# All places of the work in a transformer block's rounds set anew (steady rounds, opening, last batch)

## The chip, the cores and the metric

One NeuronCore of a Trainium2 chip (trn2). The metric is the device time of one execution in microseconds (us); several executions are timed and the median is given. Beside them stands one profiled execution, from which all rows below are taken.

## What is computed

The input x has 16 batches of 512 rows of 128 channels. A feed-forward layer, an attention layer and the same feed-forward layer follow each other, each on the normalised rows and each added to its input:

```
x = x + 0.5 * ffn(layernorm(x))
x = x + attn(layernorm(x))
x = x + 0.5 * ffn(layernorm(x))

ffn(x)  = x @ quantize_int4(kernel) + bias + (x @ a) @ b
attn(x) : 16 heads of 64; keys and values from a latent of 32 channels,
          causal mask, softmax over the 512 keys, projection back to 128
```

The feed-forward weights are folded into one 128x128 matrix before the first batch. The query and key products of a head are folded into a 128x32 matrix, so that a score is a product with the latent, and split into a high and a low part in fp32r.

## The kernel before, in words

The five engines run programs of their own, each a loop over rounds t = -2 to 16. A round has 44 places, u = 0 to 43. In a steady round every engine works on four batches at once:

- **the scores of batch t**: at each place TensorE makes one score block (`score(u)`, lines L912 and L916) into one of two PSUM banks, and ScalarE takes its exponential (L748), `e0` to `e43`. Score u waits until exponential u - 2 has freed its bank. TensorE then weighs the latents with the exponentials (`weigh_latents`, L952, 16 steps g, j), and sums rows for the denominators (L925, `weigh_ones`); GpSimd adds the exponentials of a group of heads ahead of that (`add_probs`, L625).
- **the row maxima of batch t + 1**: 38 units v (`max_unit`, L988 on TensorE into a ring of three banks, L1244 on VectorE, 0.6 us each); two of them, half of the heads each, end in a transpose (L973, L1234) and a DMA of 32x128 values into the query stack (`place_max`, L451). The scores of a half wait for that DMA.
- **the front of batch t + 2**: nine units of the first feed-forward layer, norms, keys and queries (`front_unit`, L1018 to L1035), each into the one bank `aux`. Units 4 to 7 make the queries of four groups of heads. Of each, ScalarE copies the high part (`front_copy`, L782) and VectorE takes the low part (`q_low`, L1351). When the second group is done (place `LOW_AT[3]`), the queue of SyncE issues 12 DMAs that stack these queries (`stack_queries(0)`, L419), and then, in its own order, `place_max(0)` for the next round's first score.
- **the tail of batch t - 1**: denominators inverted and spread (L1272, L1279), the scaling on GpSimd (L632), four projections (`project_out`, L1079) into `aux`, the sum with the first layer's output on VectorE (L1325, place `TAIL_SUM_AT`), its statistics (L1218 and L1224, place `TAIL_STATS_AT`), a transpose and a product (`tail_unit`, L1092 and L1095), and the output (L1332).

`aux` is used in turn by the front units, the projections and the tail units. Each user waits for the one before it to be read out. The first projection (place `PROJECT_AT[0]`) waits for front unit 4's low part (place `LOW_AT[2]`), and front unit 5 waits for the tail's sum.

Each piece has its place from tables of numbers at the head of the file; every engine runs through u = 0 to 43 and issues what has that place, in a fixed order within a place. A place of 44 or more lies in the next round. Nothing reorders this at run time: an instruction that waits holds all behind it on its engine. The tables have three sets: for steady rounds, for the opening (rounds -2 and -1, names with OPENING and FIRST), and for the last batch (names with LAST).

In the opening, round -1 makes the maxima units of batch 0 (33 of 38) beside the front of batch 1; after each unit a filler matmul runs (`keep_awake`, L1042). GpSimd takes the low parts there. ScalarE writes mask rows into the second query stack in four copies (`mask_queries`, L717, places `MASK_AT`), and the first score of batch 0 waits for all of them. The last batch has no other batch beside it: in round 16 only its last weighings, its denominators and its tail are left (`closing` on VectorE). Every `weigh_ones` that is placed in round 16 first waits for the last exponential and runs four filler matmuls (`stay_busy_by_columns`, L1063).

Of the kernel before, what the change touches and what calls it, by code (L numbers as in the profile page):

```python
# [112 lines left out]
def nth(par):  # L113

    return DMA // 2, DMA - DMA // 2 * par


def scores_by(s):
# [7 lines left out]
    8, 8, 8, 10, 11, 11, 13, 14, 15, 15, 17, 18, 19, 20, 21, 23, 23, 24, 28, 28, 29, 31, 32, 33, 34, 35, 36, 37, 37,  # L126
    38, 39, 39, 40, 42, 44, 45, 45, 50]
FIRST_MAX_AT = [
    4, 4, 4, 4, 6, 11, 11, 12, 12, 12, 12, 16, 16, 18, 18, 19, 19, 19, 23, 23, 25, 25, 28, 32, 34, 34, 36, 36, 39,
    40, 40, 41, 42, 44, 45, 46, 46, 50]  # L130
FRONT_AT = [1, 4, 12, 16, 19, 30, 33, 37, 41]
PROJECT_AT = [21, 22, 25, 27]
TAIL_AT = [35, 43]
WEIGH_AT = [[9, 9, 9, 13], [17, 21, 21, 21], [32, 34, 34, 34], [47, 50, 50, 50]]
ONES_AT = [21, 34, 50, 50]
# [5 lines left out]
FRONT_ACT_AT = [3, 7, 13, 17, 20, 31, 34, 38, 42]  # L141
NORM_AT = [9, 9, 9, 9]
TAIL_ACT_AT = 36
READ_AT = [16, 30, 37, 50]

SUM_AT = 4
STATS_AT = 6
LOW_AT = [14, 17, 21, 31, 34, 39]
TAIL_SUM_AT = 27
TAIL_STATS_AT = 28  # L150
OUT_AT = 43
NEXT_STATS_AT = 21
INVERT_AT = 6
SPREAD_AT = [8, 9, 14, 18]

SCALE_AT = [14, 15, 22, 22]
ADD_AT = [[7, 9, 19], [27, 30, 30], [41, 41, 44], [45, 46, 48]]
FIRST_RSTD_AT = 28
RSTD_AT = 4
TAIL_RSTD_AT = 34  # L160
BIAS_AT = 1
TAIL_BIAS_AT = 30


OPENING_FRONT_AT = [0, 2, 6, 13, 18, 19, 27, 36, 41]
OPENING_FRONT_ACT_AT = [0, 9, 22, 30, 32, 35, 37, 40, 41]
OPENING_NORM_AT = [8, 12, 13, 14]
OPENING_SUM_AT = 1
OPENING_STATS_AT = 3
OPENING_LOW_AT = [25, 26, 27, 30, 37, 38]  # L170
OPENING_NEXT_STATS_AT = 24
OPENING_FIRST_RSTD_AT = 40
OPENING_RSTD_AT = 7
OPENING_BIAS_AT = 4

LAST_ADD_AT = [[10, 22, 22], [22, 24, 25], [28, 29, 34], [40, 40, 42]]
# [33 lines left out]
def macaron_block(nc, x, wq, wkv_down, wk_up, wv_up, wout, ffn_w, ffn_bias, ffn_a, ffn_b, out):  # L210
    ctx = ExitStack()
    with ctx:
# [301 lines left out]
        def _(pool):  # L514
# [59 lines left out]
            def one_round(t, par):  # L574
# [76 lines left out]

                for u in range(SCORES):
# [22 lines left out]
                    if is_first(t) and u == 0:  # L675
                        pool.wait_ge(bias_loaded, DMA)
                        nc.gpsimd.tensor_scalar(half_bias[:], half_bias[:], 0.5, None, ALU.mult).then_inc(const_made, 1)
                        pool.wait_ge(const_made, 7)
                    if prep and u == bias_at:
                        wait_batch(pool, f_full, t, 2, F_UNITS, 1)  # L680
                        nc.gpsimd.tensor_tensor(x_in[:, par], x_in[:, par], half_bias[:, None, :].broadcast_to([P, TT, D]),
                                                ALU.add).then_inc(xb_made, 1)
# [4 lines left out]
                    if end and u == TAIL_BIAS_AT:  # L687
                        first = 0
                        if not attend:
                            first = TT - 1  # L690
                            pool.wait_ge(x2_closed, first)
                            wait_batch(pool, out_stored, t, -1, DMA, 0)
                            nc.gpsimd.tensor_tensor(x2b[:, 0:first], x2[:, 0:first],
                                                    half_bias[:, None, :].broadcast_to([P, first, D]), ALU.add).then_inc(x2b_begun, 1)
                            pool.wait_ge(x2b_begun, 1)
                        wait_batch(pool, t_free, t, -1, T_UNITS, 1)
                        wait_batch(pool, out_stored, t, -1, DMA, 0)
                        nc.gpsimd.tensor_tensor(x2b[:, first:], x2[:, first:], half_bias[:, None, :].broadcast_to([P, TT - first, D]),
                                                ALU.add).then_inc(x2b_made, 1)
# [4 lines left out]
        def _(act):  # L704
# [27 lines left out]
            def one_round(t, par):  # L732
# [67 lines left out]

                for u in range(SCORES):
                    if t == -1 and u in MASK_AT:
                        mask_queries(1, MASK_AT.index(u))
                    if end and u == TAIL_ACT_AT:
                        wait_batch(act, t_full, t, -1, T_UNITS, 2)
                        nc.scalar.activation(x2_t[:], aux[:], ACT.Copy).then_inc(t_free, 1)
# [334 lines left out]
        def _(dve):  # L1141
# [67 lines left out]
            def one_round(t, par):  # L1209
# [101 lines left out]
                for u in range(SCORES):  # L1311
                    if prep and u == sum_at:
                        wait_batch(dve, f_full, t, 2, F_UNITS, 2)
                        wait_batch(dve, xb_made, t, 2, 1, 1)
                        wait_batch(dve, x1_saved[par], t, 0, *nth(par))
                        wait_batch(dve, f_rstd_made, t, 2, 2, 1)
                        for i in range(TT):
                            last = nc.vector.scalar_tensor_tensor(x1[:, par, i, :], aux[:, i * P:(i + 1) * P],
                                                                  f_rstd[:, 0, i:i + 1], x_in[:, par, i, :],
                                                                  ALU.mult, ALU.add)  # L1320
                        last.then_inc(f_free, 1)
# [91 lines left out]
```

## Time and profile before

| | |
|---|---|
| three timed runs, us | 785.49, 784.26, 780.52; median 784.26 |
| the profiled execution, us | 784.9 |
| its span from first to last instruction, us | 783.2 |
| mean granted TensorE clock | 0.984 of 2.4 GHz |
| TensorE matmul busy | 764.2 us, 98% |
| VectorE / ScalarE / GpSimd busy | 80% / 65% / 83% |

The span can be read as an opening up to about 62 us (the first score), 14 rounds with all or nearly all four stages, and a last part without a next batch from about 730 us. Steady rounds take some 45 us each. Matmuls are pipelined and their ends are modelled, so busy matmul time also holds short waits between them.

### The profile page before, as it was taken

How to read it: one execution, taken by the hardware profiler on the slowest of the kernel's cores; microseconds unless marked ns; L12 is line 12 of the kernel's file. 1: busy time of each engine (PE TensorE's matmuls, PEld its weight loads, DVE VectorE, ACT ScalarE, POOL GpSimd, SP SyncE). 2: the span in 40 equal slices, each digit the busy share in tenths (PEclk: the TensorE clock that was granted, in tenths of full speed). 3: DMA queues.
4: the chain of work that ended last, by engine and by line, in shares of the span. 5: the costliest groups of instructions: out<-in, count | busy, mean ns of one | idle time of the engine just before them, and what ended most of it. 6: DMA issues, size and time to landing. Idle time of an engine off the chain costs nothing.

```text
span 783.2 us, 20715 instructions
## 1 busy us (share of the span) xinstructions
PE 764.2 (98%) x7632; PEld 591.6 (76%) x7632; DVE 623.7 (80%) x1983; ACT 507.5 (65%) x995; POOL 650.0 (83%) x449
## 2 busy tenths in 40 slices
PE   8799999999999999999999999999999999999997
PEld 6687777777787778778787877878787777867665
DVE  4678788788878888898878879887887889776635
ACT  6277676667667676767657666676766676655670
POOL 5626788898899989888998989889898988888892
PEclk7789999999999999999999999999999999999999
DMA  5647270734636172553627154372616445360101
GB/s 117 159 98 173 58 181 25 163 86 106 148 80 147 47 159 73 123 130 82 164 48 162 50 134 120 84 169 61 148 47 150 101 110 130 75 150 3 30 1 42
DMA packets 81141, 80.99 MB, mean 103 GB/s; under 512 B 16064, under 2 KB 68560, under 8 KB 81040
## 3 DMA queue, kind: packets, MB, share of 16 engines
q1 hardware_dynamic: 80480, 78.47, 43.0%
q10 hardware_dynamic: 560, 1.20, 0.6%
q8 instruction: 61, 1.00, 0.5%
q14 instruction: 40, 0.33, 0.1%
HBM read 9.90 MB, written 8.39 MB: 23 GB/s over the span
## 4 chain that ended last, share of the span: by engine, by line
PE 79%; SPq 7%; DVE 6%; DMA 2%; ACT 2%; issue 2%; POOL 1%; DVEq 0%; POOLq 0%; ACTq 0%
PE bank L952 16%; PE bank L988 14%; PE bank L916 12%; PE bank L925 7%; PE bank L912 7%; PE bank L1079 7%; SPq L419 7%; DMA q_stack<-max_t 2%; PE bank L1021 2%; PE bank L1018 2%; PE bank L1030 2%; PE bank L1032 2%; PE bank L1031 2%; PE bank L1095 1%; PE bank L1042 1%
## 5 line engine op out<-in xcount | busy, mean ns | idle before, releaser
L1244 DVE TENSOR_REDUCE strip_max<-bank 128x8 f32<-128x512 f32 (+1 forms) x384 | 254.1, 683 | 51.6 <-PE bank L988 50.7
L748 ACT ACTIVATE later_probs<-bank 128x512 f32<-128x512 f32 x384 | 216.3, 601 | 65.5 <-PE bank L916 41.0
L748 ACT ACTIVATE first_probs<-bank 128x384 f32<-128x384 f32 (+1 forms) x320 | 157.5, 513 | 137.0 <-PE bank L916 69.5
L625 POOL TENSOR_TENSOR totals<-totals,later_probs 128x1024 f32<-128x1024 f32 x124 | 227.6, 1835 | 12.5 <-ACT later_probs L748 0.4
L625 POOL TENSOR_TENSOR totals<-first_probs,later_probs 128x1536 f32<-128x1536 f32 x62 | 215.6, 3478 | 26.1 <-ACT later_probs L748 26.1
L988 PE MATMUL bank<-keys,q_stack 118*128 118x512 f32 (+7 forms) x1024 | 215.1, 303 | 1.8 <-DVE maxima L1244 1.7
L916 PE MATMUL bank<-q_stack,keys 119*128 119x384 f32 (+1 forms) x448 | 185.2, 422 | 2.4 <-ACT later_probs L748 1.3
L988 PEld LDWEIGHTS bank<-keys,q_stack 118*128 118x128 f32 x1024 | 177.1, 191 | 12.6 <-DVE maxima L1244 2.2
L1244 DVE TENSOR_REDUCE maxima<-bank 128x1 f32<-128x512 f32 (+1 forms) x192 | 128.1, 681 | 2.1 <-PE bank L988 1.9
L912 PE MATMUL bank<-q_stack,keys 119*128 119x256 f32 x512 | 114.0, 304 | 2.8 <-DMA q_stack<-max_t 2.6
L916 PEld LDWEIGHTS bank<-q_stack,keys 119*128 119x128 f32 x448 | 82.7, 188 | 44.9 <-ACT first_probs L748 16.2
L912 PEld LDWEIGHTS bank<-q_stack,keys 119*128 119x128 f32 x512 | 82.4, 189 | 33.3 <-ACT later_probs L748 17.2
L952 PE MATMUL bank<-later_probs,lat 128*32 128x384 f32 (+2 forms) x1536 | 99.9, 383 | 0.0
L632 POOL TENSOR_TENSOR y_norm<-y_sb,y_norm 128x512 f32<-128x512 f32 x60 | 76.7, 1291 | 15.6 <-DVE y_norm L1279 15.6
L952 PEld LDWEIGHTS bank<-later_probs,lat 128*32 128x32 f32 x1536 | 43.1, 109 | 53.5 <-issue 35.1
L1079 PE MATMUL bank<-w_out,y_norm 128*128 128x128 f32 x512 | 69.1, 278 | 1.3 <-POOL y_norm L614 1.3
L1079 PEld LDWEIGHTS bank<-w_out,y_norm 128*128 128x128 f32 x512 | 63.1, 191 | 5.7 <-issue 3.8
L952 PE MATMUL bank<-first_probs,lat 128*32 128x512 f32 x512 | 66.7, 593 | 0.3 <-ACT y_sb L754 0.2
L1279 DVE STREAM_SHUFFLE y_norm<-den_inv 128x128 f32<-128x128 f32 x240 | 54.2, 308 | 0.5
L925 PE MATMUL bank<-totals,row_ones 128*32 128x128 f32 x1512 | 50.4, 273 | 0.0
L754 ACT ACTIVATE y_sb<-bank 128x512 f32<-128x512 f32 x64 | 38.4, 601 | 16.9 <-PE bank L952 16.9
L1351 DVE TENSOR_TENSOR q_low<-bank,q_high 128x512 fp32r<-128x512 f32 x60 | 41.0, 684 | 9.1 <-ACT q_high L782 9.1
(157 smaller groups left out, 917.0 us busy)
## 6 DMA issues: line engine op xcount, KB each, us to landing
q_stack<-q_high SPq DMA_DIRECT2D x252, 128.0 KB, 2.4
q_stack<-q_low SPq DMA_DIRECT2D x128, 128.0 KB, 2.4
x_in<-in_L_attn_x_bld_dram SPq DMA_DIRECT2D x16, 256.0 KB, 3.3
out_dram<-x SPq DMA_DIRECT2D x16, 256.0 KB, 3.5
x_back<-out_dram SPq DMA_DIRECT2D x16, 256.0 KB, 3.0
out_dram<-x2b SPq DMA_DIRECT2D x15, 256.0 KB, 2.3
keys<-keys_staged SPq DMA_DIRECT2D x16, 192.0 KB, 2.9
keys<-keys_staged SPq DMA_DIRECT2D x32, 96.0 KB, 2.6
```

The lines of the kernel that those rows point to most:

```text
L419: eng.dma_start(dst.bitcast(F32), src[e * LD:(e + 1) * LD, half].rearrange("c w o q -> c (w o q)").bitcast(F32)).then_inc(q_stacked[half][ ...
L625: nc.gpsimd.tensor_tensor(total, first_probs[g % 2][:, :, P:] if j == 1 else total, probs_of(g, j)[:], ALU.add).then_inc(added, 1)
L632: nc.gpsimd.tensor_tensor(y_norm[:, g, :], y_sb[:, g, :], y_norm[:, g, :], ALU.mult).then_inc(y_normed, 1)
L748: nc.scalar.activation(out, score_bank(t, u)[:, 0:heads * cols].rearrange("p (e q) -> p e q", e=heads), ACT.Exp).then_inc(exp_done, 1)
L912: last = nc.tensor.matmul(out, strips(par, KM, OWN[w]), q_stack[par][:, pair:pair + HG, w, of, :], start=True, stop=True)
L916: last = nc.tensor.matmul(bank[:, 0:heads * (n - P)], strips(par, KM, LATER[j]), q_stack[par][:, pair + e:pair + e + heads, 2 * (j + 1):SU ...
L925: last = nc.tensor.matmul(den_bank[e * LD:(e + 1) * LD, 0:P], row_ones[:, row:row + LD], of[:, e, :], start=start, stop=stop)
L952: last = nc.tensor.matmul(y_bank[e * LD:(e + 1) * LD, j * P:L], lat[(par + off) % 2][:, j, :], probs_of(g, j)[:, e, 0:L - P * j], start=(j ...
L988: last = nc.tensor.matmul(bank[:, col:col + n], queries, strips((par + off) % 2, KC, SEEN[w]), start=True, stop=True)
L1079: last = nc.tensor.matmul(out_tile(t, i), y_norm[:, g, i * P:(i + 1) * P], w_out[:, g, :], start=(g == 0), stop=(g == G - 1))
L1244: nc.vector.tensor_reduce(out, bank[:].rearrange("q (b k) -> q b k", k=strip), AX.X, ALU.max).then_inc(a_free, 1)
L1279: last = nc.vector.stream_shuffle(y_norm[:, g, i * P:(i + 1) * P], den_inv[:], [g * TT + i] * LD)
```

## The change

The tables of places get new numbers, for steady rounds, opening and last batch. Beside them some code is put into functions of its own (`add_front`, `add_tail`, `make_out`, `take_low`, `front_stats`, `tail_stats` on VectorE, `halve_bias`, `add_bias`, `tail_bias` on GpSimd, `tail_copy` on ScalarE), which are called from the same points with the same waits, so that the line numbers of the kernel after are some 12 to 25 higher. The lines of the tables of which the prediction speaks:

```diff
-FRONT_AT = [1, 4, 12, 16, 19, 30, 33, 37, 41]
-PROJECT_AT = [21, 22, 25, 27]
+FRONT_AT = [2, 4, 11, 15, 19, 29, 32, 37, 41]
+PROJECT_AT = [23, 25, 26, 27]
...
-LAST_WEIGH_AT = [[10, 13, 13, 14], [21, 21, 25, 31], [33, 40, 40, 40], [42, 50, 51, 52]]
-LAST_ONES_AT = [33, 40, 49, 54]
+LAST_WEIGH_AT = [[8, 14, 14, 14], [20, 24, 24, 24], [30, 37, 37, 37], [55, 61, 62, 66]]
+LAST_ONES_AT = [37, 45, 65, 92]
...
-MASK_AT = [23, 31, 36, 37]
+MASK_AT = [16, 21, 30, 34]
...
-LOW_AT = [14, 17, 21, 31, 34, 39]
-TAIL_SUM_AT = 27
-TAIL_STATS_AT = 28
+LOW_AT = [14, 16, 21, 30, 34, 39]
+TAIL_SUM_AT = 28
+TAIL_STATS_AT = 32
...
-NEXT_STATS_AT = 21
+NEXT_STATS_AT = 20
...
-OPENING_FRONT_AT = [0, 2, 6, 13, 18, 19, 27, 36, 41]
+OPENING_FRONT_AT = [2, 5, 9, 20, 24, 25, 27, 29, 39]
...
-LAST_ADD_AT = [[10, 22, 22], [22, 24, 25], [28, 29, 34], [40, 40, 42]]
+LAST_ADD_AT = [[16, 21, 31], [31, 32, 32], [35, 35, 40], [43, 60, 61]]
```

The moved code keeps its form, as here on VectorE:

```diff
                 for u in range(SCORES):
                     if prep and u == sum_at:
-                        wait_batch(dve, f_full, t, 2, F_UNITS, 2)
...
-                        last.then_inc(f_free, 1)
+                        add_front()
```

**First place: VectorE in a steady round, between the tail's sum and the low part of the second query group.** `x<-bank,x_back` is the sum, BN_STATS and BN_AGGR of `t_stats` are its statistics, TENSOR_REDUCE are maxima units, `q_low` is the low part on which SyncE's queue waits. Before:

```order
L1325 TENSOR_TENSOR x<-bank,x_back 128x512
L1244 TENSOR_REDUCE maxima<-bank 128x1
L1244 TENSOR_REDUCE strip_max<-bank 128x8
L1218 BN_STATS t_stats<-x 128x6 x4
L1224 BN_AGGR t_mv<-t_stats 128x2 x4
L1244 TENSOR_REDUCE strip_max<-bank 128x4
L1351 TENSOR_TENSOR q_low<-bank,q_high 128x8x64
```

And after, the same stretch (the sum is L1343 there, the low part L1374):

```order
L1343 TENSOR_TENSOR x<-bank,x_back 128x512
L1260 TENSOR_REDUCE strip_max<-bank 128x8
L1260 TENSOR_REDUCE strip_max<-bank 128x4
L1374 TENSOR_TENSOR q_low<-bank,q_high 128x8x64
L1260 TENSOR_REDUCE strip_max<-bank 128x8
L1250 TENSOR_SCALAR max_t<-bank 32x128
L1260 TENSOR_REDUCE maxima<-bank 128x1
L1234 BN_STATS t_stats<-x 128x6 x4
L1240 BN_AGGR t_mv<-t_stats 128x2 x4
```

One maxima unit now stands ahead of the sum, and the eight instructions of the statistics stand behind the low part.

**Second place: VectorE in a steady round, ahead of the first projection.** `f_stats<-x_in` are the input statistics of batch t + 3, the `q_low` here is that of the first query group, for which the first projection waits. Before:

```order
L1279 STREAM_SHUFFLE y_norm<-den_inv 128x128 x4
L1244 TENSOR_REDUCE strip_max<-bank 128x8
L1244 TENSOR_REDUCE maxima<-bank 128x1
L1351 TENSOR_TENSOR q_low<-bank,q_high 128x8x64
L1244 TENSOR_REDUCE strip_max<-bank 128x8
L1218 BN_STATS f_stats<-x_in 128x6 x4
L1224 BN_AGGR f_mv<-f_stats 128x2 x4
```

And after:

```order
L1260 TENSOR_REDUCE strip_max<-bank 128x8
L1295 STREAM_SHUFFLE y_norm<-den_inv 128x128 x4
L1260 TENSOR_REDUCE maxima<-bank 128x1
L1234 BN_STATS f_stats<-x_in 128x6 x4
L1240 BN_AGGR f_mv<-f_stats 128x2 x4
L1374 TENSOR_TENSOR q_low<-bank,q_high 128x8x64
L1260 TENSOR_REDUCE strip_max<-bank 128x8
```

The statistics stand ahead of the low part instead of behind it. On TensorE the first projection moves back too, behind two more scores and two maxima units.

**Third place: TensorE in round -1, around the transposes of the normalised rows** (`bank<-identity,xn`, front unit 2 of batch 1). `keys,q_stack` are maxima units of batch 0, `bank<-identity` is a filler matmul. Before:

```order
L988 MATMUL bank<-keys,q_stack 128x512
L1042 MATMUL bank<-identity 128x128
L1018 MATMUL bank<-identity,xn 128x128 x4
L988 MATMUL bank<-keys,q_stack 128x448
L988 MATMUL bank<-keys,q_stack 128x64
L1042 MATMUL bank<-identity 128x128
L988 MATMUL bank<-keys,q_stack 128x384
L988 MATMUL bank<-keys,q_stack 128x128
```

And after:

```order
L1004 MATMUL bank<-keys,q_stack 128x512
L1058 MATMUL bank<-identity 128x128
L1004 MATMUL bank<-keys,q_stack 128x448
L1004 MATMUL bank<-keys,q_stack 128x64
L1058 MATMUL bank<-identity 128x128
L1004 MATMUL bank<-keys,q_stack 128x384
L1004 MATMUL bank<-keys,q_stack 128x128
L1058 MATMUL bank<-identity 128x128
L1034 MATMUL bank<-identity,xn 128x128 x4
```

Two maxima units stand ahead of the transposes instead of behind them.

In the last batch, the row sums of group 1 and the first weighing of group 3 stand in round 15 before, and in round 16 after; so two `weigh_ones` lie in round 16 instead of one, each with its four filler matmuls.

## Rows read from the trace of the kernel before

**Rows 1.** The page's part 1: busy us, share of the span, instructions of an engine.

```profile
PE 764.2 (98%) x7632; PEld 591.6 (76%) x7632; DVE 623.7 (80%) x1983; ACT 507.5 (65%) x995; POOL 650.0 (83%) x449
```

**Rows 2.** The chain of waits, whole span: start us, us, what; one same step per round.

```profile
107.88 1.42 PE bank L925 x48
...
423.62 1.31 PE bank L925 x48
...
468.44 1.50 PE bank L925 x48
...
513.93 1.31 PE bank L925 x48
...
693.26 1.31 PE bank L925 x48
```

**Rows 3.** The chain of waits from 355 to 373 us, the end of a steady round.

```profile
355.60 0.91 PE bank L1079 x8
...
356.53 0.69 DVE x L1325
...
358.42 0.79 DVE t_stats L1218 x4
...
359.34 0.38 DVE t_mv L1224 x4
...
360.21 0.69 DVE q_low L1351
...
363.53 1.59 SPq L419
...
369.68 2.29 DMA q_stack<-max_t
...
372.02 0.50 PE bank L912 x2
```

**Rows 4.** Who waited for whom on TensorE, whole span: us in total, times, longest.

```profile
PE bank L912 <- DMA q_stack<-max_t: 2.6, 7, 0.8
```

**Rows 5.** Instructions in order of time, 348.5 to 352.5 us: start, us, engine.

```profile
349.58 0.68 DVE L1351 TENSOR_TENSOR q_low<-bank,q_high 128x512 fp32r<-128x512 f32 x1
...
350.68 1.16 PE L1079 MATMUL bank<-w_out,y_norm 128*128 128x128 f32 x8
350.78 0.86 DVE L1218 BATCH_NORM_STATS2 f_stats<-x_in 128x6 f32<-128x128 f32 x4
...
351.78 0.62 DVE L1224 BATCH_NORM_AGGREGATE f_mv<-f_stats 128x2 f32<-128x6 f32 x4
```

**Rows 6.** Instructions in order of time, opening, 36 to 62 us.

```profile
39.33 1.54 PE L1018 MATMUL bank<-identity,xn 128*128 128x128 f32 x4 [0.91 <-ACT xn L761]
...
41.34 0.69 DVE L1244 TENSOR_REDUCE strip_max<-bank 128x8 f32<-128x512 f32 x1 [1.91 <-PE bank L988]
...
48.01 1.91 ACT L717 ACTIVATE q_stack<-first_probs 22x2048 fp32r<-22x2048 f32 x1
...
49.94 0.60 ACT L782 ACTIVATE q_high<-bank 128x512 fp32r<-128x512 f32 x1
...
54.56 1.15 SPq L419 DMA_DIRECT2D q_stack<-q_high  x2
...
61.67 0.48 PE L912 MATMUL bank<-q_stack,keys 119*128 119x256 f32 x2
```

**Rows 7.** Busy us of each engine in two stretches of the opening, then PEclk.

```profile
35.00:40.00 5.00, 2.37 (x13) 1.59 (x11) 4.25 (x14) 1.31 (x4) 1.69 (x4) 0.86 0.94 211
40.00:45.00 5.00, 5.00 (x21) 4.66 (x21) 2.77 (x4) 3.33 (x4) 1.27 (x1) 0.50 0.82 203
```

**Rows 8.** Instructions in order of time, last batch, 761 to 769 us.

```profile
763.39 0.60 ACT L748 ACTIVATE later_probs<-bank 128x512 f32<-128x512 f32 x1 [0.54 <-PE bank L912]
...
764.18 1.07 PE L1063 MATMUL bank<-w_out,identity 128*32 128x512 f32 x8
...
768.35 0.96 DVE L1272 RECIPROCAL den_inv<-bank 128x128 f32<-128x128 f32 x1 [2.94 <-PE bank L925]
```

More of the change, by code:

```diff
@@ L687, in one_round @@
                     if end and u == TAIL_BIAS_AT:
[L688 to L699, printed above, removed]
+                        tail_bias()
             rounds(pool, one_round)
@@ L799, in front_copy, with tail_copy @@
                                              ACT.Copy).then_inc(f_free, 1)
+                def tail_copy():
+                    wait_batch(act, t_full, t, -1, T_UNITS, 2)
+                    nc.scalar.activation(x2_t[:], aux[:], ACT.Copy).then_inc(t_free, 1)
                 for u in range(SCORES):
@@ new lines, in add_front @@
+                def add_front():
+                    wait_batch(dve, f_full, t, 2, F_UNITS, 2)
+                    wait_batch(dve, xb_made, t, 2, 1, 1)
+                    wait_batch(dve, x1_saved[par], t, 0, *nth(par))
+                    wait_batch(dve, f_rstd_made, t, 2, 2, 1)
+                    for i in range(TT):
+                        last = nc.vector.scalar_tensor_tensor(x1[:, par, i, :], aux[:, i * P:(i + 1) * P],
+                                                              f_rstd[:, 0, i:i + 1], x_in[:, par, i, :],
+                                                              ALU.mult, ALU.add)
+                    last.then_inc(f_free, 1)
@@ new lines, in add_tail, with make_out @@
+                def add_tail():
+                    wait_batch(dve, t_full, t, -1, T_UNITS, 1)
+                    wait_batch(dve, x1_loaded, t, -1, DMA, DMA)
+                    nc.vector.tensor_tensor(x2[:].rearrange("p i d -> p (i d)"), aux[:],
+                                            x1_back[:].rearrange("p i d -> p (i d)"), ALU.add).then_inc(t_free, 1)
+                def make_out():
+                    wait_batch(dve, t_full, t, -1, T_UNITS, 3)
+                    wait_batch(dve, x2b_made, t, -1, 1, 1)
+                    wait_batch(dve, t_rstd_made, t, -1, 1, 1)
+                    for i in range(TT):
+                        last = nc.vector.scalar_tensor_tensor(x2b[:, i, :], aux[:, i * P:(i + 1) * P],
+                                                              t_rstd[:, i:i + 1], x2b[:, i, :], ALU.mult, ALU.add)
+                        if not attend and i == TT // 2 - 1:
+                            last.then_inc(half_out, 1)
+                    last.then_inc(t_free, 1)
@@ L1340, in one_round @@
                                                 ALU.subtract).then_inc(f_free, 1)
-                    if prep and not low_by_pool(t) and u == low_at[1]:
+                    elif n == 1:
                         wait_batch(dve, kh_made, t, 2, 1, 1)
```

148 lines of the change are left out of this document (77 added, 71 removed).

## The prediction, made before the result was known

> **What bounds the kernel now.** I read the page's engine totals first. TensorE's matmuls are busy 98% of the span [rows 1], the next engines 83% and 80%. A reader should see two things: no other engine is the bound over the whole, and only some 19 us without a matmul are left (783.2 less 764.2). Then the chain of waits over the whole span. It goes along TensorE nearly everywhere, and one step of it, the row sums of group 0, comes back once per round [rows 2]. From the first to the last of these rows it is 693.26 - 107.88 = 585.38 us for 13 rounds, 45.03 us each. The rounds aren't alike: 468.44 - 423.62 = 44.82, and the next one 513.93 - 468.44 = 45.49. So there is a round in which hardly anything is waited for, and 13 such rounds would take 582.7, 2.7 us less than now.
>
> What the others wait for stands in the chain at the end of a round [rows 3]. It leaves TensorE at the last projection (ends 356.51), goes over VectorE's sum, the statistics of that sum and the low part of the second query group (ends 360.90), then over 12 DMA issues in SyncE's queue to 369.68, where the maxima's DMA is issued. That takes 2.29, and the first score of the next round starts at 372.02. The list of waits gives this one 2.6 us in 7 rounds on TensorE [rows 4]. It is TensorE's longest entry, and small: order can win little in steady rounds, unless it shortens what TensorE does itself.
>
> The page on traces speaks on this. By the Trainium skill (Perfetto Trace Analysis, Identifying the Most-Contended Engine) matmul occupancy says little of the headroom, and weight loads are the better measure. Here those are 76% against 98% [rows 1]. By the one number 19 us are left to win in all, by the other far more; I let the waits decide, not either share.
>
> **The change, steady rounds.** The set of matmuls of a round stays as it is, so TensorE's own work doesn't change, and only waits can.
>
> - *The low part of query group 2 comes earlier.* Before, sum (starts 356.53), two maxima units, statistics, one unit, low part. The statistics take 358.42 to 359.72, 1.30 us [rows 3]; they now stand behind. A maxima unit moves ahead of the sum, where VectorE waits for the projection anyhow: another 0.60 (357.82 to 358.42 is one unit, from the same rows). The last projection comes one unit later on TensorE (0.24). That makes 1.30 + 0.60 - 0.24 = 1.66 at most; the high copy by ScalarE will then be what comes last, so I take 1.3, between 1.0 and 1.66. SyncE's 12 issues (8.8 us, one of them 1.59 instead of 0.59) and the DMA follow 1.3 us earlier. The longest excess of a round is 45.49 - 44.82 = 0.67, so the first score no longer waits: -2.7.
> - *The first front unit stands one score later* (`FRONT_AT[0]`). It needs `aux`, which the output of the round before reads until shortly after the new round's first score. A round that starts without the wait above meets this one. No row prices it; I bound it by 0 and by one score, 0.2 us a round, and take 0.1 times 13: -1.3.
> - *The input statistics stand ahead of the low part for which the first projection waits.* That low part ends at 350.26 and the projection starts at 350.68 [rows 5], so 0.42 us of cover. The statistics run 350.78 to 352.40, with a wait inside; without it they are as the others, 1.30. Low part: 350.26 + 1.30 + 0.1 = 351.7, to 351.9 with the wait. The projection stands behind two more scores and two more units (some 0.4 + 0.24 + 0.2 + 0.24 = 1.1 us): 351.8. So between 0 and 0.15 us a round, I take 0.05, times 13: +0.6.
> - The tail's statistics, now later, are needed by the output only, at the round's end; GpSimd's root for it has 8 us. The bias add on GpSimd comes behind one more addition (2.4 us), and the front sum behind one more weighing (0.65): the norms after it wait 0.8 us longer at most, and ScalarE has exponentials to do there. The new groups of weighings on TensorE have as many changes between small and large matmuls as the old. Nothing for these, 0 to 0.1 us a round.
>
> Steady rounds: -2.7 - 1.3 + 0.6 = **-3.4** (bounds -5.3 to -0.7).
>
> **The opening.** From 37 to 62 us VectorE's maxima units, 0.6 us each, are the longest chain, and it has gaps. The longest is 1.91 us [rows 6]: TensorE waits for the norms (0.91) with the transposes, and the next maxima unit stands behind them. Two units now stand ahead: two of 0.6 fit in the gap, -1.2. Between the transposes and the next front unit one unit less stands, which brings ScalarE's copies forward. There a mask copy of 1.91 runs until 49.92 and the query copy behind it starts at 49.94 [rows 6], though its matmuls had ended some 0.5 us before; that mask copy moves behind the next front units: -0.5. The rest is what the following front units, each waiting for ScalarE to free `aux`, gain by being earlier; I add 0.8 (0 to 1.5). Then the first score would start 2.5 earlier, at 59.2 instead of 61.67. There a new limit stands: of the four mask copies three now lie between and behind the query copies, and the last ends about 59.2 by the same durations. Hence **-2.5** (0 to -4). The queue of SyncE, which starts its 12 issues at 54.56 when the third low part is there, goes the same 1.6 us or more earlier, so that batch 1's keys are not late.
>
> The clock in this stretch: 2.37 of 5 us busy, then 0.50 granted, that is 1.2 GHz [rows 7]. By the Trainium skill (TensorE: Matmul & The Clock Gate, Part 1) it is idleness that halves the clock, and the trace agrees. The stretch before it doesn't change, so I leave this as it is.
>
> **The last batch.** Work is moved from round 15 into 16: row sums of group 1 and the first weighing of group 3. ScalarE's last exponentials come earlier, since GpSimd's additions and the weighings no longer hold them: I reckon some 3 us before the 763.39 of now [rows 8]. But TensorE has then 0.65 + 1.9 of moved work and four more filler matmuls (1.07 us, rows 8) left behind the last exponential. 3.0 against 3.6 less some overlap: **0** (-2 to +1.5). From the last denominators (VectorE at 768.35) on, nothing changes.
>
> **Sum.** The profiled execution took 784.9 (span 783.2 and 1.7 around it): 784.9 - 3.4 - 2.5 + 0 = 779.0. It lies 0.6 above the median of the runs, 784.26, so against that median I say 778.4.
>
> **The rivals.**
>
> *The first projection waits (slower).* VectorE gets to the low part of the first query group later than I say: besides the statistics its high copy stands behind one more exponential. The trace is for it in that my margin is 0.1 us; against it, that VectorE has idle time in every round (80% busy). It costs from the first 0.1 us on, in each of 13 rounds, and makes the kernel slower than before from 5.9 / 13 = 0.45 us. With all of the 1.30 uncovered less the present 0.42 cover and more of the same, 1.0 a round: 778.4 + 13 = 791.4.
>
> *The wait goes and the rounds stay as long.* ScalarE works without a gap at a round's end, and TensorE is held there by exponentials; an earlier first score is then given back a few us later. For it: a round without the wait at its start was not the shortest. Against: 44.82 was reached several times. Steady rounds then give 0.5, the opening its 2.5: 784.9 - 3.0 - 0.6 = 781.3.
>
> *TensorE's clock stays up in the opening.* Two more units at 38.5 to 40 us. If they kept the clock at 2.4 GHz, the 5 us of full work at half clock [rows 7] would take about 2.5, of which VectorE lets 2.2 through: 776.2. Against it: the fall comes behind a stretch that doesn't change.
>
> *The rounds get shorter than the shortest now.* The order also takes away waits too short to be listed, in scores that wait for exponentials. 0.3 a round times 13: 778.4 - 3.9 = 774.5. For it: a matmul's modelled end hides such waits in the 98%.
>
> **How the numbers follow.** Forecast (776 to 781) 0.44; projection waits 0.09; rounds stay 0.20; clock 0.12; shorter rounds 0.15. Likeliest time 778.4. For 8 in 10 the range runs from the shorter rounds with something of the opening, 773, to beyond the case in which rounds stay as they are, 784; most of the first rival is left out. A measurement of this kernel can tell about 1% from no change, 7.8 us, so faster means under 776.4 and slower over 792.1. Faster: the last two rivals and the edge of the forecast, 0.27 + 0.06 = 0.33. Slower: most of the first rival, 0.07. Within 1%: 0.60.
>
> **What would show it right or wrong.** In the profile after: the wait of the first score for the maxima's DMA is gone from TensorE's list; the recurring step of the chain comes every 44.7 to 44.8 us; SyncE's queue is no longer in the chain of steady rounds; the first projection shows at most 0.1 us behind VectorE's low part. The first score starts at 59 to 60 us, right behind the last mask copy. In the last batch the last exponential starts about 3 us earlier against the start of its round, and the last denominators don't. Wrong would be: rounds over 45.0 with a new entry for the projection, or a first score at 61 or later.

## The result, and the profile after

| | before | after |
|---|---|---|
| median of 13 timed runs, us | 782.67 (780.52 to 787.65) | 777.19 (775.72 to 782.57) |
| ratio after to before | | 0.9937, 95% interval 0.9913 to 0.996 |
| span of the profiled execution, us | 783.2 | 774.5 |
| its mean granted TensorE clock | 0.984 | 0.995 |

The time fell by 5 to 5.5 us, 0.6% (0.4 to 0.9%): inside the band of 1% that the prediction called no change, 1.2 us from the predicted 778.4. A second measurement of the changed kernel (seven executions, beside 21 of the kernel before) gave 777.77 against 783.5, ratio 0.9933 (0.9909 to 0.9957). The profiled executions differ by more, 8.7 us, and a part of that is luck of the clock (below). So where the clock matters, before is compared with the profile of the second measurement (span 777.6): up to 38 us its clock ran as that of before.

The page's part 1 of the kernel after, as [rows 1]:

```profile
PE 758.5 (98%) x7638; PEld 586.5 (76%) x7638; DVE 624.6 (81%) x1983; ACT 508.3 (66%) x995; POOL 649.6 (84%) x449
```

Six matmul records more (eight for the fillers of the second `weigh_ones` in round 16, two of `keep_awake` less), and still 98%: the shares say nothing on what was gained. The chain's shares by engine, from the page's part 4, first of before and then of after, do:

```profile
PE 79%; SPq 7%; DVE 6%; DMA 2%; ACT 2%; issue 2%; POOL 1%; DVEq 0%; POOLq 0%; ACTq 0%
```

```profile
PE 93%; DVE 3%; ACT 2%; POOL 1%; issue 1%; DVEq 0%; POOLq 0%; ACTq 0%
```

SyncE's queue and the DMA have left the chain: the end of a round no longer runs over the stacking of queries. The recurring step, in the chain of waits of after (start us, us, what; [rows 2] before):

```profile
102.09 1.31 PE bank L941 x48
147.03 1.31 PE bank L941 x48
191.89 1.31 PE bank L941 x48
...
684.85 1.31 PE bank L941 x48
726.24 1.31 PE bank L941 x48
```

Thirteen rounds take 684.85 - 102.09 = 582.76, 44.83 each (before 45.03), and nearly every one 44.86 (191.89 - 147.03, for one; the step before round 14 is 43.93, since maxima and front run out there). Before, the shortest full rounds took 44.82 and the longer ones up to 45.81; now nearly all are like the shortest, but none of the full rounds is shorter than 44.84. Experiment 3 shows why not. TensorE's longest waits after, total, times, longest:

```profile
PE bank L1095 <- POOL y_norm L614: 1.3, 2, 0.7
PE bank L846 <- POOL neg_half L517: 1.2, 1, 1.2
```

The entry of [rows 4], the first score waiting for the maxima's DMA, isn't there. The end of the steady round, in order of time on VectorE, ScalarE and SyncE's queue ([rows 3] in chain form before):

```profile
349.75 0.69 DVE L1343 TENSOR_TENSOR x<-bank,x_back 128x512 f32<-128x512 f32 x1 [0.20 <-PE bank L1095]
350.35 1.28 DVE L1260 TENSOR_REDUCE strip_max<-bank 128x8 f32<-128x512 f32 x2
351.56 0.60 ACT L794 ACTIVATE q_high<-bank 128x512 fp32r<-128x512 f32 x1
352.19 0.69 DVE L1374 TENSOR_TENSOR q_low<-bank,q_high 128x512 fp32r<-128x512 f32 x1 [0.55 <-ACT q_high L794]
...
353.05 1.15 SPq L419 DMA_DIRECT2D q_stack<-q_high  x2
...
361.78 0.53 SPq L451 DMA_DIRECT2D q_stack<-max_t  x1
```

From the sum to the low part it is now 2.44 us (352.19 - 349.75) against 3.68 before (360.21 - 356.53), 1.24 less. VectorE idles 0.55 ahead of the low part for ScalarE's high copy, so that copy is what comes last now.

**Where the time came from.** The recurring step cuts both spans into the same pieces (before, and the second profile of after). Opening to the first score: 61.67 and 58.31, -3.4. From there to the first such step: 46.21 and 47.06, +0.9. Thirteen rounds: 585.38 and 582.63 (105.37 to 688.00), -2.8. Round 14: 42.02 and 41.40, -0.6. The rest: 47.92 and 48.2, +0.3. Together -5.6, the difference of the spans. Of the -3.4, about 0.9 is clock and not order: between the normalisation of batch 1 and the first score TensorE ran 6.8 us at half clock before and 3.4 in the second profile of after, and in the old opening 6.8 instead of 3.4 made 0.94 (22.98 and 22.04, experiment 4).

### The profile page after: what moved, and what is told of

Same layout as the page of the kernel before. It is cut to its first block, busy times and chain, and to the rows that moved or that the text cites. A ratio compares the mean times of both kernels' runs of the same rounds, so it can differ in the third digit from the quotient of the medians.

```text
span 774.5 us, 20727 instructions
## 1 busy us (share of the span) xinstructions
PE 758.5 (98%) x7638; PEld 586.5 (76%) x7638; DVE 624.6 (81%) x1983; ACT 508.3 (66%) x995; POOL 649.6 (84%) x449
## 4 chain that ended last, share of the span: by engine, by line
PE 93%; DVE 3%; ACT 2%; POOL 1%; issue 1%; DVEq 0%; POOLq 0%; ACTq 0%
PE bank L968 19%; PE bank L1004 18%; PE bank L932 15%; PE bank L928 9%; PE bank L941 8%; PE bank L1095 7%; PE bank L1046 3%; PE bank L1048 2%; PE bank L1047 2%; PE bank L1034 2%; PE bank L1037 2%; PE bank L1111 2%; PE bank L1108 1%; ACT later_probs L760 1%; PE bank L1051 1%
## 5 line engine op out<-in xcount | busy, mean ns | idle before, releaser
L1260 DVE TENSOR_REDUCE strip_max<-bank 128x8 f32<-128x512 f32 (+1 forms) x384 | 249.9, 682 | 17.3 <-PE bank L1004 16.3
L760 ACT ACTIVATE first_probs<-bank 128x384 f32<-128x384 f32 (+1 forms) x320 | 150.8, 511 | 105.1 <-PE bank L932 70.5
L1004 PE MATMUL bank<-keys,q_stack 118*128 118x512 f32 (+7 forms) x1024 | 212.6, 305 | 1.9 <-DVE maxima L1260 1.0
L932 PE MATMUL bank<-q_stack,keys 119*128 119x384 f32 (+1 forms) x448 | 177.3, 419 | 1.3 <-ACT first_probs L760 0.8
L1004 PEld LDWEIGHTS bank<-keys,q_stack 118*128 118x128 f32 x1024 | 168.7, 190 | 10.8 <-DVE maxima L1260 1.7
L928 PE MATMUL bank<-q_stack,keys 119*128 119x256 f32 x512 | 111.8, 301 | 0.3 <-ACT later_probs L760 0.2
L968 PE MATMUL bank<-later_probs,lat 128*32 128x384 f32 (+2 forms) x1536 | 104.8, 383 | 0.0
L1095 PE MATMUL bank<-w_out,y_norm 128*128 128x128 f32 x512 | 68.4, 277 | 1.7 <-POOL y_norm L614 1.3
L1095 PEld LDWEIGHTS bank<-w_out,y_norm 128*128 128x128 f32 x512 | 64.3, 191 | 4.9 <-issue 2.2
L1374 DVE TENSOR_TENSOR q_low<-bank,q_high 128x512 fp32r<-128x512 f32 x60 | 40.8, 679 | 7.6 <-ACT q_high L794 7.5
```

Source lines behind the costliest of these rows:

```text
L760: nc.scalar.activation(out, score_bank(t, u)[:, 0:heads * cols].rearrange("p (e q) -> p e q", e=heads), ACT.Exp).then_inc(exp_done, 1)
L928: last = nc.tensor.matmul(out, strips(par, KM, OWN[w]), q_stack[par][:, pair:pair + HG, w, of, :], start=True, stop=True)
L932: last = nc.tensor.matmul(bank[:, 0:heads * (n - P)], strips(par, KM, LATER[j]), q_stack[par][:, pair + e:pair + e + heads, 2 * (j + 1):SU ...
L968: last = nc.tensor.matmul(y_bank[e * LD:(e + 1) * LD, j * P:L], lat[(par + off) % 2][:, j, :], probs_of(g, j)[:, e, 0:L - P * j], start=(j ...
L1004: last = nc.tensor.matmul(bank[:, col:col + n], queries, strips((par + off) % 2, KC, SEEN[w]), start=True, stop=True)
L1095: last = nc.tensor.matmul(out_tile(t, i), y_norm[:, g, i * P:(i + 1) * P], w_out[:, g, :], start=(g == 0), stop=(g == G - 1))
```

## The experiments

Each variant is compared with executions of the kernel before (or of the changed kernel, 777.77) on the same chip; "13 rounds" is the length between the first and the 14th recurring step of its profile.

**1. The steady tables alone, and the opening tables alone.** The kernel before with the new MAX, FRONT, PROJECT, LOW, TAIL, ADD and other steady tables, but the old ones for opening and last batch:

```diff
-FRONT_AT = [1, 4, 12, 16, 19, 30, 33, 37, 41]
+FRONT_AT = [2, 4, 11, 15, 19, 29, 32, 37, 41]
...
-TAIL_STATS_AT = 28
+TAIL_STATS_AT = 32
```

> The kernel before with the new steady tables alone; opening and last batch keep their old places. If the steady part of the gain is the first score's wait for the maxima's DMA, that wait is gone from TensorE's list, each round takes about 44.85 us as in the kernel after, the 13 rounds from group 0's row sums to the last of them take about 583.3 instead of 585.4 us, and the time falls by 2.0 to 2.8 us. Rival, that the whole gain is made in the opening: rounds as in the kernel after, but nothing of it at the end, within 0.5 us of before. Rival, that the tables only work together: slower than before by 1 us or more.

Measured: 781.99 against 782.33, ratio 0.9995 (0.997 to 1.002), so between 2.3 us less and 1.6 more: the 2.0 to 2.8 us expected aren't to be seen in the time, though its rounds are as expected. The second kernel takes only the opening's tables and `MASK_AT`:

```diff
-MASK_AT = [23, 31, 36, 37]
+MASK_AT = [16, 21, 30, 34]
...
-OPENING_FRONT_AT = [0, 2, 6, 13, 18, 19, 27, 36, 41]
+OPENING_FRONT_AT = [2, 5, 9, 20, 24, 25, 27, 29, 39]
```

> The kernel before with the new opening tables alone. If the opening's order is worth 2.5 us by itself, the first score starts 2.5 us earlier than in a run of before with the same clock in its first 50 us, and the time falls by 2 to 3 us; the 13 steady rounds take 585 to 586 us as before. Rival, that the first score at 55.4 us after against 61.7 before was the clock of the two profiled executions and nothing else: time within 0.5 us of before over the rounds, and the first score anywhere from 55 to 62 us. Rival, that the order is worth the whole 6.6 us: time 6 us less.

Measured: 779.14 against 782.33, ratio 0.9966 (0.9939 to 0.9994). So the opening is worth something by itself, between 0.5 and 4.8 us. Its 13 rounds take 584.46, 0.9 less than before, and TensorE still lists the first score's wait:

```profile
PE bank L912 <- DMA q_stack<-max_t: 1.7, 4, 0.9
```

The steady tables give their gain in the rounds (688.35 - 105.71 = 582.64 in the first kernel), and lose part of it ahead of them (first score at 58.75 to the first such step 46.96, before 46.21) and in the last batch. From the first score of the last batch to VectorE's last denominators, the rows of the steady-only kernel, of after, and of before are these:

```profile
723.65 0.48 PE L912 MATMUL bank<-q_stack,keys 119*128 119x256 f32 x2
...
764.06 0.96 DVE L1272 RECIPROCAL den_inv<-bank 128x128 f32<-128x128 f32 x1 [2.94 <-PE bank L925]
```

```profile
720.15 0.48 PE L928 MATMUL bank<-q_stack,keys 119*128 119x256 f32 x2
...
759.62 0.96 DVE L1288 RECIPROCAL den_inv<-bank 128x128 f32<-128x128 f32 x1 [3.45 <-PE bank L941]
```

```profile
729.09 0.48 PE L912 MATMUL bank<-q_stack,keys 119*128 119x256 f32 x2
```

That is 40.41, 39.47 and, with [rows 8], 39.26. New steady tables with the old last batch cost 1.15; the new last tables bring 0.94 of it back. Their worth is a repair. The new last weighings and row sums in the kernel before, with nothing else moved, gave no time: that kernel deadlocks, with engines left waiting for the denominators. So the last batch has no measurement of its own.

**2. One number alone: the tail's statistics.**

```diff
-TAIL_STATS_AT = 28
+TAIL_STATS_AT = 32
```

> The kernel before with one number changed, TAIL_STATS_AT 28 to 32: the tail's statistics stand behind the low part of the second query group. If the chain sum, statistics, low part, 12 issues, DMA, first score is what made rounds uneven, this alone takes the wait away: no wait of TensorE for the maxima's DMA, every round 44.8 to 44.9 us, the 13 rounds 582.8 to 583.5 us, time 2.0 to 2.8 us less. Rival, that ScalarE's end of the round holds TensorE anyway: the wait moves, the 13 rounds stay at 585 us.

Measured: 793.21 against 782.33, ratio 1.0128 (1.0078 to 1.0178). Slower by 10 to 11 us, which no theory had. Its lists of waits lead to the cause: TensorE's longest entry, then GpSimd's, then the same pair in the kernel before:

```profile
PE bank L925 <- POOL totals L625: 9.2, 13, 1.0
```

```profile
POOL t_var L582 <- DVE t_mv L1224: 46.6, 16, 4.4
```

```profile
POOL t_var L582 <- DVE t_mv L1224: 5.0, 13, 1.3
```

GpSimd takes the root of these statistics at place `TAIL_RSTD_AT` (34), ahead of additions that TensorE's row sums need. Nothing overtakes a waiting instruction, so GpSimd stood up to 4.4 us before the root in each round, and the additions behind it came late, as its rows in order of time show:

```profile
367.00 0.23 POOL L582 TENSOR_SCALAR t_var<-t_mv 128x4 f32<-128x4 f32 x1 [2.91 <-DVE t_mv L1224]
367.31 1.04 POOL L584 TENSOR_TENSOR t_rstd<-t_var,neg_half 128x4 f32<-128x4 f32 x1
...
368.32 3.49 POOL L625 TENSOR_TENSOR totals<-first_probs,later_probs 128x1536 f32<-128x1536 f32 x1
```

The change moves that root to 42, behind the additions that have place 41. So the two numbers belong together, and a run took both.

```diff
-TAIL_STATS_AT = 28
+TAIL_STATS_AT = 32
...
-TAIL_RSTD_AT = 34
+TAIL_RSTD_AT = 42
```

> The kernel before with TAIL_STATS_AT 28 to 32 and, this time, TAIL_RSTD_AT 34 to 42 with it, so that GpSimd's root no longer holds the additions. Theory A (the loss of 11.7 us in the run with the statistics alone came from the root held in front of the additions): the loss is gone, the low part of the second query group stands some 0.6 us earlier than before (as the variant of the changed kernel with the statistics set back showed with the other sign), the wait of the first score is mostly gone, rounds of 44.6 to 44.9, 13 of them 582 to 583.5, so 2 to 3 us less than before, about 780.5. Theory B (the later statistics themselves make the rounds long): rounds stay near 45.7, 793.

Measured: 779.87 against 782.02, ratio 0.9973 (0.9954 to 0.9993); 13 rounds in 582.41 (106.25 to 688.66), 2.97 less than before. The recurring step in its chain:

```profile
106.25 1.42 PE bank L925 x48
...
688.66 1.31 PE bank L925 x48
```

Theory A holds: two numbers give as much in the 13 rounds as all steady tables together. The other way round, in the changed kernel:

```diff
-TAIL_STATS_AT = 32
+TAIL_STATS_AT = 29
```

> The changed kernel with TAIL_STATS_AT set back from 32 to 29, so that the tail's statistics (1.3 us) stand ahead of the low part of the second query group again; GpSimd's root stays late (42). Theory of the prediction (the statistics ahead of the low part make SyncE's queue and with it the maxima's DMA late): the low part is 1.0 to 1.3 us later, the wait of the first score is back in part of the rounds (0.2 to 0.7 us each), 2 to 3 us more than the changed kernel. Rival (the root's place on GpSimd made the wait, since it held the additions): the time stays.

Measured: 777.8 beside 777.77 of the changed kernel; 13 rounds in 583.06, 0.30 more. The expected 2 to 3 us didn't come back, and by the time alone this is what the rival said. The rows say more. The low part starts 3.68 behind the sum before, 3.15 in the kernel with the pair, 3.11 here and 2.44 in the changed kernel. So the statistics alone move it by 0.53 or 0.67, and not by their own 1.3. The first score's weight load (engine PEld) waits for the maxima's DMA accordingly, in the kernel before, with the pair, and here:

```profile
PEld bank L912 <- DMA q_stack<-max_t: 3.9, 7, 1.0
```

```profile
PEld bank L912 <- DMA q_stack<-max_t: 0.7, 4, 0.2
```

```profile
PEld bank L928 <- DMA q_stack<-max_t: 0.5, 2, 0.3
```

In the changed kernel the entry is missing. Less than half of the lead already takes most of the wait away; the rest buys little. The root at 42 with the statistics still at 28 wasn't run, so a share of the root in the 2.97 isn't excluded. Against a large one speaks that TensorE's weight loads waited only 0.4 us for GpSimd's additions before, and 0.4 with the pair.

**3. The two moves that the prediction priced at 0.1 and 0.05 a round.** In the changed kernel, each for itself:

```diff
-NEXT_STATS_AT = 20
+NEXT_STATS_AT = 21
```

> The changed kernel with one number set back: NEXT_STATS_AT 20 to 21, so that the input statistics stand behind the low part of the first query group again. Theory A (this move makes the first projection wait in every round, about 0.2 us, since the shortest round grew from 44.65 to 44.85): rounds of 44.65, 13 x 0.2 = 2.6 us less than the changed kernel, about 774.5 us. Theory B (the 0.2 a round is something else, such as one weighing more that changes tile size): rounds stay at 44.85, same time within 0.5 us.

Measured: **774.16** (773.29 to 775.93) beside 777.77 (776.61 to 779.78); ratio to before 0.9884 (0.9856 to 0.9912). Theory A holds: 13 rounds in 579.93 (103.23 to 683.16), 2.83 less than after (expected 2.6). The medians differ by 3.6, but all six executions of this kernel had a mean clock of 0.993 or more and only four of the seven beside it did; against those four (median 777.1) it is 3.0. Nearly every round now takes 44.63, which is shorter than the shortest full round before (44.82). So in the changed kernel this move had eaten what the first front unit (below) gave, and that is why none of its rounds fell under 44.84.

Round 0, though, grew: from the first score to the first recurring step it is 47.63, in after 47.05.

The chain around the first projection (L1095 x8), in after and then in this kernel:

```profile
342.87 0.66 PE bank L941 x24
...
344.43 0.23 PE bank L1004 x2
344.66 1.13 PE bank L1095 x8
```

```profile
342.90 0.66 PE bank L941 x24
...
344.45 0.23 PE bank L1004 x2
344.69 0.92 PE bank L1095 x8
```

The step takes 1.13 instead of 0.92. No wait is listed for it: at 0.2 us a round it hides as a longer step, and in the timeline as a weight load that comes 0.17 late:

```profile
343.90 0.66 DVE L1374 TENSOR_TENSOR q_low<-bank,q_high 128x512 fp32r<-128x512 f32 x1
...
344.63 0.97 PEld L1095 LDWEIGHTS bank<-w_out,y_norm 128*128 128x128 f32 x8 [0.17 <-issue]
```

The low part ends at 344.56 and the load starts at 344.63; with the number set back the load starts at 344.44. "issue" names no releaser; the time beside the low part's end, and the run with the low part moved, do.

```diff
-FRONT_AT = [2, 4, 11, 15, 19, 29, 32, 37, 41]
+FRONT_AT = [1, 4, 11, 15, 19, 29, 32, 37, 41]
```

> The changed kernel with FRONT_AT[0] set back from 2 to 1: the first front unit stands behind the round's first score again and may wait for aux, which the output reads. The prediction gave this move 0.1 us a round (between 0 and 0.2), so it expects rounds of 44.95 and 1.3 us more than the changed kernel. Rival: the output is read out by then, and the move is worth nothing: 44.85 and the same time.

Measured: 778.53 beside 777.77; 13 rounds in 687.23 - 102.55 = 584.68, 1.92 more, 0.15 a round. The rival (worth nothing) is out by the rounds; the medians alone wouldn't tell it. The chain shows the wait at the front unit's transposes (L1034) as a step of 0.07 and a longer step, here and then in after:

```profile
322.21 0.07 issue
322.28 0.63 PE bank L1034 x4
```

```profile
321.34 0.51 PE bank L1034 x4
```

A last run tried to keep the 0.22 a round without the loss that place 21 brought in round 0:

```diff
-                next_stats_at = OPENING_NEXT_STATS_AT if t < 0 else NEXT_STATS_AT
+                next_stats_at = OPENING_NEXT_STATS_AT if t < 0 else 20 if t == 0 else NEXT_STATS_AT
```

> The changed kernel with NEXT_STATS_AT 21 (the version that won 0.22 us a round), but 20 in round 0, where the place 21 made the round 0.58 us longer (40.62 against 40.04). Expected: 13 rounds of 580.8 as there, round 0 back at 40.04, so 3.3 us less than the changed kernel, 773.6 us. Rival: round 0 gives it back in round 1, and it is 774.2 as there.

Measured: 775.19 (773.49 to 778.6) against 782.02, ratio 0.9917 (0.989 to 0.9944). 13 rounds take 579.67 (105.69 to 685.36), and from the first score (58.53) to the first recurring step it is 47.16, so round 0 came back and round 1 (44.74) didn't take it. But the timed runs don't set it apart from the simpler version.

**4. Inside the opening.** First, the two maxima units ahead of the transposes, and nothing else (`FIRST_MAX_AT`, two numbers):

```diff
-    4, 4, 4, 4, 6, 11, 11, 12, 12, 12, 12, 16, 16, 18, 18, 19, 19, 19, 23, 23, 25, 25, 28, 32, 34, 34, 36, 36, 39,
+    4, 4, 4, 4, 6, 6, 6, 12, 12, 12, 12, 16, 16, 18, 18, 19, 19, 19, 23, 23, 25, 25, 28, 32, 34, 34, 36, 36, 39,
```

> The kernel before with two maxima units of the opening (units 5 and 6 of batch 0) moved ahead of the transposes on TensorE, nothing else. The prediction gave this 1.2 us: the gap of 1.91 us on VectorE shrinks to 0.7, and the first score comes 1.2 earlier. Rival (ScalarE's copies and the front units that wait for them are the chain, and the maxima only fill): the gap shrinks to about 1, but the first score comes 0 to 0.5 us earlier.

Measured: 782.04 against 782.02, ratio 0.9984 (0.9958 to 1.001): not to be told from nothing by time. Then the opening tables with the mask copies left at their old places:

```diff
 MASK_AT = [23, 31, 36, 37]
...
-OPENING_FRONT_AT = [0, 2, 6, 13, 18, 19, 27, 36, 41]
+OPENING_FRONT_AT = [2, 5, 9, 20, 24, 25, 27, 29, 39]
```

> The kernel before with the new opening tables but the old MASK_AT: two of the four mask copies (1.91 us each) then stand behind the second and third query copy, and two behind the last front copy. Theory of the prediction (the last mask copy sets the first score): from front unit 0 of batch 1 to the first score 26.3 us in the changed kernel, at least 1.5 us more here, and the first score right behind the last mask copy. Rival (the maxima units on VectorE set it and the mask copies are beside them): the same 26.3 to 27.

Measured: 784.96 against 782.02, ratio 1.0045 (1.0026 to 1.0063). The new order of maxima and front units without the new mask places loses 2.9 instead of winning 3.2. Its last mask copies and first score, then the second profile of after:

```profile
59.09 3.70 ACT L717 ACTIVATE q_stack<-first_probs 22x2048 fp32r<-22x2048 f32 x2
...
62.85 0.79 PE L912 MATMUL bank<-q_stack,keys 119*128 119x256 f32 x2 [3.52 <-ACT q_stack L717]
```

```profile
56.35 1.91 ACT L729 ACTIVATE q_stack<-first_probs 22x2048 fp32r<-22x2048 f32 x1
...
58.31 0.50 PE L928 MATMUL bank<-q_stack,keys 119*128 119x256 f32 x2
```

In both the first score stands right behind the last mask copy (ends 62.79 and 58.26). Without the new mask places the copy is the limit, with a listed wait of 3.52. In the changed kernel it is so at most by a hair: the score follows 0.05 us later in each of its profiles, but TensorE was busy up to it and lists no wait there. The new mask places have no worth alone either: before, the last mask copy ended at 56.90, and the first score came at 61.67.

The clock confuses the lengths. Up to the start of ScalarE's normalisation of batch 1 (`xn`, L761, 38.69 before) the orders don't differ: from the end of that batch's first transposes it is 6.66 to 6.68 us in all of these profiles but one, in which half clock falls into that part. From there to the first score:

| kernel | xn to first score, us | half clock within (PEclk 0.50 in stretches of 1 us) |
|---|---|---|
| before | 22.98 | 6.8 us (38.6 to 45.5) |
| steady tables alone (old opening) | 22.04 | 3.4 us |
| statistics and root (old opening) | 20.67 | none (its fall ended at 35.8) |
| two units ahead | 20.50 | none |
| after, second profile | 19.79 | 3.4 us |
| after; opening alone | 19.17; 19.18 | none |
| new opening, old mask places | 24.24 | 3.4 us |

The rows for the third and fourth line of the table, `xn` and the first score of each:

```profile
39.39 1.65 ACT L761 ACTIVATE xn<-x,f_shift,f_rstd 128x128 f32<-128x128 f32 x4 [6.95 <-POOL f_shift L601]
...
60.06 0.48 PE L912 MATMUL bank<-q_stack,keys 119*128 119x256 f32 x2
```

```profile
36.55 1.65 ACT L761 ACTIVATE xn<-x,f_shift,f_rstd 128x128 f32<-128x128 f32 x4 [6.04 <-POOL f_shift L601]
...
57.05 0.48 PE L912 MATMUL bank<-q_stack,keys 119*128 119x256 f32 x2
```

At full clock the new opening is 20.67 - 19.17 = 1.50 us shorter, with 3.4 us of half clock in both 22.04 - 19.79 = 2.25, though the two falls don't lie at quite the same point. The two units alone give 20.67 - 20.50 = 0.17: the rival of that experiment came true. VectorE's gap did close, from 1.57 to 0.38, but the next front unit (keys) moved only from 4.81 to 4.65 behind `xn`, since it now waits 0.69 for GpSimd's low part of the normalised rows. The rest is read from the rows and wasn't tested apart. Most of it lies where the mask copy stood: between ScalarE's copy of the keys and the first query copy, it is 3.17 in the old order and 2.26 in the new, without it.

## Why the prediction was right, and where it wasn't

**The forecast case came true**, with the signs it named: wait and queue gone, first score 58.3, rounds of 44.83, last exponential about 3 us earlier in its round with the denominators unchanged. That exponential is the last of this run of five, in the last batch of after:

```profile
749.60 2.55 ACT L760 ACTIVATE later_probs<-bank 128x512 f32<-128x512 f32 x5
```

It ends 32.00 after the batch's first score, and before ended 34.90 after it (763.99 - 729.09). Point by point:

- *The wait of the first score, -2.7.* The pair of statistics and root alone gives -2.97, and the low part is 1.24 earlier behind the sum (I said 1.3, ScalarE's copy coming last). Right in size, but the statistics give only 0.53 to 0.67 of that and not most of it. Two more things the step missed. First, it spoke of the root's 8 us of room as if that came with the move, and it comes only with `TAIL_RSTD_AT` 42; with 34 the same move costs 10 to 11 us. Second, the other steady moves nearly suffice without the statistics.
- *The first front unit, -1.3.* Measured -1.92 (0.15 a round, inside the bounds 0 to 0.2).
- *The first projection, +0.6.* This is the term that failed: measured +2.83, 0.22 a round against 0.05, outside my bounds of 0 to 0.15. The low part was reckoned to end at the projection's start. It did, but the projection's weight load wants it earlier: that load starts 0.03 ahead of the matmul and was 0.17 late. So a margin of nothing was a wait. The rival "first projection waits" had the right mechanism with a price over four times too high (1.0 against 0.22 a round), and the rival "rounds get shorter than the shortest now" comes true only with this number set back (44.63).
- *Sum of steady rounds, -3.4.* Measured -2.6 to -2.8 for the 13. Of the single measurements -2.97, -1.92 and +2.83 make -2.06, and 0.6 is left to the other moves, which weren't tried apart; the three were measured in different kernels, so the sum is rough. Of the -2.6, 0.65 lies in the last of the thirteen, in which maxima and front run out (44.58 before, 43.93 after). Round 14 gave 0.6 more (with all steady tables; the pair alone leaves it at 42.03) and round 0 took 0.9; the prediction priced neither. The rival in which rounds stay as long is out.
- *The opening, -2.5.* At the same granted clock -1.5 (full) to -2.25 (with a fall), and the new limit named for it (last mask copy, reckoned at 59.2) was found at 58.3, if level with TensorE's own work. Of its parts, the two units were worth 0.17 and not 1.2. The step that failed is that VectorE's maxima units are the longest chain from 37 us on: over most of that stretch the chain ran over the front units with their copies on ScalarE and GpSimd, and the gap on VectorE was room. The mask places were worth more than the 0.5 written beside them: 0.9 between key copy and query copy, and without them the other moves lose. That the total of the opening fits is in part luck.
- *The clock in the opening.* The prediction left it as it was, and gave 0.12 to the rival in which it stays up. That rival came true in part. Of 69 runs of the kernel before, 6 had a mean granted clock of 0.993 or more; of 20 runs of the kernel after, 13. Of ten runs each: 6 with the opening tables alone, 4 with the two units alone, 2 with the steady tables alone, 2 with statistics and root, none with the new opening and the old mask places, whose wait for them brings a late fall of its own. On the same chips the kernel before had 4 of 19 beside the first, 2 of 29 beside the second and 0 of 21 beside the second measurement of after (4 of 7). So the new order does keep TensorE at 2.4 GHz more often. Runs of that clock took 779.7 before and 776.9 after (medians), runs below 0.99 784.5 and 779.8. The differences are 2.8 and 4.7: a part of the 5.5 us is thus a clock that falls less, and the places alone give about 3 to 5.
- *The last batch, 0.* Measured +0.2 from first score to last denominators: the last exponential ends 2.9 earlier, and from there to the last denominators it is 7.47 instead of 4.36 (759.62 - 752.15 and 768.35 - 763.99), 3.1 more. I had said 3.0 against 3.6 less some overlap.

The error in one term (2.2 too cheap) and the unpriced loss in round 0 (0.9) were covered by gains it had priced too low or not at all (0.6 in front unit 0, 0.6 in round 14, the clock). The total fits better than its parts. The starting point had luck too: 784.26 was the median of three executions, and thirteen gave 782.67. The forecast fall was 5.9, the measured one 5 to 5.5.

## What to carry to other kernels

When an order without reordering is changed, move the consumer of a result with its producer, on every engine: one number alone cost some 10 us here that gains 3 with its mate. Ask of each matmul behind a late operand when its weight load starts, and leave the load some tenths; below the resolution of the list of waits such a loss shows only as one chain step that is longer in every round. Before pricing a gap on one engine, follow the chain behind it: 1.2 us of gap closed on VectorE gave 0.17 here. Afterwards set back each moved number that costs in the profile: undoing one of the moved numbers made the best version, 774.2 us.

## What the runs showed of the hardware

**The granted clock in the opening differs from run to run of one kernel**, and its times follow it: in the second measurement of after, the four executions with a mean clock of 0.995 took 776.61 to 777.77, the three below 0.99 took 778.61 to 779.78. These are two profiles of the same changed kernel (busy us of PE, PEld, DVE, ACT, POOL, then PEclk, DMA share, GB/s), first the one and then the other:

```profile
5.00:10.00 5.00, 4.71 (x22) 4.38 (x23) 3.00 (x17) 4.95 (x4) 3.09 (x4) 1.00 1.07 242
...
40.00:45.00 5.00, 4.81 (x34) 4.28 (x33) 4.18 (x8) 3.22 (x5) 1.78 (x3) 1.00 0.68 175
```

```profile
5.00:10.00 5.00, 3.69 (x20) 3.23 (x21) 2.97 (x17) 4.95 (x4) 3.08 (x4) 0.80 1.06 248
...
40.00:45.00 5.00, 5.00 (x32) 4.75 (x30) 3.67 (x7) 3.44 (x5) 1.29 (x1) 0.78 0.75 191
```

One has its first score at 55.04, the other at 58.31, and that 3.27 covers the 3.1 us between their spans. Comparing openings from single profiles without their clock rows would have told a gain of 6.6 us where the order gave 1.5 to 2.3. The fall follows idleness here too: with the first score waiting 3.52 us for the mask copies, the clock went from 1.00 in 55 to 60 us to these two stretches:

```profile
60.00:65.00 5.00, 2.15 (x7) 2.01 (x8) 0.57 (x1) 3.78 (x4) 0.00 (x0) 0.75 0.76 174
65.00:70.00 5.00, 5.00 (x25) 4.84 (x24) 3.55 (x13) 1.92 (x5) 1.28 (x1) 0.57 0.90 196
```

By the Trainium skill (TensorE: Matmul & The Clock Gate, Part 1) the gate runs freely beside the kernel, so that the same kernel finds it in another phase each time. The two profiles, which part already at 5 to 10 us (1.00 and 0.80), agree with that. The Trainium skill (same page, same part) puts the penalty of the clock's ramp at under 1% of a typical kernel's span. Here the seven times spread over 3.2 us, 0.4%, but 1% was all there was to find in this case.

**The losing engine isn't the one that shows the loss.** With the statistics alone moved, GpSimd waited 2.9 us each time (46.6 in 16), TensorE's listed waits for it were 9.2 us, and the kernel lost 10 to 11. TensorE's list pointed at GpSimd's additions; only GpSimd's own list named what had held them.
